# Two attention layers on one core: new tables of jobs, feed-forward products handed out in pairs, and a flag kept in a register

## What is computed

```python
x = L0_attn_x                       # (8, 512, 128)
xn = layernorm(x)
x = x + L0_attn(xn) + L0_ffn(xn)    # 16 heads, two softmax maps per head (dimension 4)
xn = layernorm(x)
x = x + L1_attn(xn) + L1_ffn(xn)    # 16 heads (dimension 8) with rotary positions

# L0_attn: o = softmax(q1 k1 / 2) v - lam * softmax(q2 k2 / 2) v; per-head rms norm; o @ W_proj + b
# L0_ffn:  both operands rounded to a 6-bit grid in blocks of 32 with a scale each, one product, bias
# L1_attn: softmax(rope(q) rope(k) / sqrt(8)) v; then @ w_proj
# L1_ffn:  h = 2 * relu(s0 * [x, -x] @ K0); h = 2 * relu(s1 * h @ K1); s2 * h @ K2
#          K0 (256 x 512), K1 (512 x 512), K2 (512 x 128) have entries +1 and -1
```

## Time and profile before

| what | us |
|---|---|
| median of three runs | 836.71 |
| the profiled execution, its own time | 837.15 |
| its span, first to last instruction | 835.4 |
| ACT busy | 760.7 (91% of the span) |
| PE busy | 749.4 (90%) |
| DVE busy | 551.5 (66%) |
| POOL busy | 64.2 (8%) |

### The profile page before, as it was taken

The page is one execution under the profiler, slowest core; times in us unless marked ns, Lnnn a source line. Parts: engine busy times, 40 slices in busy tenths (PEclk is TensorE's granted clock), DMA queues, the critical chain, the costliest instruction groups (busy, mean ns, idle before and its releaser), DMA issues.

```text
span 835.4 us, 17855 instructions
## 1 busy us (share of the span) xinstructions
PE 749.4 (90%) x6751; PEld 245.8 (29%) x6751; DVE 551.5 (66%) x1186; ACT 760.7 (91%) x856; POOL 64.2 (8%) x84
## 2 busy tenths in 40 slices
...
GB/s 104 182 38 176 77 90 194 73 2 76 140 75 129 14 77 139 103 102 14 115 133 138 33 52 140 82 159 2 102 128 81 122 2 123 81 1 88 128 13 14
DMA packets 45934, 73.99 MB, mean 89 GB/s; under 512 B 7344, under 2 KB 23344, under 8 KB 45712
## 3 DMA queue, kind: packets, MB, share of 16 engines
...
q10 hardware_dynamic: 64, 0.10, 0.0%
...
## 4 chain that ended last, share of the span: by engine, by line
PE 47%; ACT 29%; DVE 12%; issue 11%; DVEq 0%; DMA 0%; ACTq 0%; SPq 0%
ACT probs L807 28%; PE ps_pv L981 18%; PE ps_s L962 11%; PE ps_misc L828 6%; PE ps_misc L832 6%; PE ps_misc L833 4%; PE ps_misc L821 1%; ACT ff_out L759 1%; DVE pv_sb L1509 1%; DVE h_lo L1218 0%; ACT ff_out L761 0%; DVE tmp L1276 0%; DVE qk_rest L1269 0%; DVE qk_thirds L1266 0%; DVE xn L1093 0%
## 5 line engine op out<-in xcount | busy, mean ns | idle before, releaser
L807 ACT ACTIVATE probs<-ps_s 128x1024 f32<-128x1024 f32 x768 | 723.5, 1053 | 40.6 <-PE ps_s L962 40.0
L981 PE MATMUL ps_pv<-probs,v_aug 128*32 128x512 f32 x3072 | 411.4, 608 | 14.5 <-DVE pv_sb L1509 7.7
L962 PE MATMUL ps_s<-q_ab,k_ab 32*128 32x512 bf16 x896 | 88.9, 387 | 22.9 <-ACT probs L807 22.1
L962 PE MATMUL ps_s<-q_c,k_c 32*128 32x512 f32 (+1 forms) x640 | 81.0, 495 | 27.3 <-ACT probs L807 26.2
L981 PEld LDWEIGHTS ps_pv<-probs,v_aug 128*32 128x32 f32 x3072 | 61.7, 108 | 106.3 <-issue 79.1
L1216 DVE CAST h_hi<-ff_out 128x512 fp32r<-128x512 f32 x64 | 27.3, 427 | 93.7 <-ACT ff_out L759 91.2
L832 PE MATMUL ps_misc<-h_hi,k_w 128*128 128x512 f32 x192 | 85.9, 447 | 0.4 <-DVE tmp L1276 0.3
L1509 DVE STREAM_TRANSPOSE pv_sb<-ps_pv 128x512 f32<-128x512 f32 x48 | 34.4, 717 | 69.3 <-PE ps_pv L981 67.4
L833 PE MATMUL ps_misc<-h_lo,k_w 128*128 128x512 f32 x192 | 75.7, 395 | 0.0
L962 PEld LDWEIGHTS ps_s<-q_c,k_c 32*128 32x128 f32 (+1 forms) x640 | 30.9, 181 | 136.7 <-ACT probs L807 113.7
L962 PEld LDWEIGHTS ps_s<-q_ab,k_ab 32*128 32x128 bf16 x896 | 22.8, 91 | 158.6 <-ACT probs L807 127.0
...
## 6 DMA issues: line engine op xcount, KB each, us to landing
...
```

The costliest lines, as they stand in the source:

```text
L807: nc.scalar.activation(probs[:, U.slot(s), 2 * half:2 * half + 2], ps_s[:, 2 * pair:2 * pair + 2], ACT.Exp, bias=0.0 if U.first else -SCAL ...
L962: ins = nc.tensor.matmul(ps_s[:, bank, :], k[row:row + n, slot, c * P:(c + 1) * P], q[row:row + n, slot, :], start=True, stop=True)
L981: ins = nc.tensor.matmul(ps_pv[32 * j:32 * j + 32, :], v_aug[:, U.v, c, a:a + 32], probs[:, U.slot(s), j, :], start=c == 0 and not odd, st ...
```

## The change

The three tables are written anew. An item `ff1` or `ff2` is now one block (two matmuls) with its number in the item, and `ff1_b`, `ff2_b` are the last block alone; so each output is four items that may stand in different steps. Each waits only for the split of the block that it reads (`ff_split`), where before it waited for all four. PE loads layer 0's flag once and keeps it in a register, so `exact0` of sequences 1 to 7 only branches. In layer 1's general path (skipped with the given data) the masked copy of q goes to a part of `q_c` that is free, instead of `h1_hi`, after a wait that this needs, since `h1_hi` may now be read meanwhile. The tables, of which two items of `LOOP` stand for the rest, and the code:

```diff
 LOOP = [
-    12: [("bias", 1), ("quant_mm", 1)], 14: [("exact0", 1), ("ff2", -1)]},
+    12: [("bias", 1)],
+     13: [("quant_mm", 1)], 14: [("exact0", 1)], 15: [("regroup", 0, "B", 0), ("ff2", -1, 0)]},
...
+        def masked(way, b):
+
+            if way == 1:
+                slot = operands(unit("C", b))[2]
+                return q_c[:, slot:slot + PARTS]
+            return h0_hi if way == 0 else q_masked
...
                 elif name in ("ff1", "ff1_b"):
                     c = slice(args[0] * P, (args[0] + 1) * P)
-                    pe.wait_ge(ff_split, 2 * (2 * NF * b + NF))
-                    for f in ((0, 1) if name == "ff1" else (2, 3)):
-                        ins = products(ps, k1_w[:, f, c], h0_hi[:, f, :], h0_lo[:, f, :], f == 0, f == NF - 1)
+                    f = NF - 1 if name == "ff1_b" else args[1]
+                    pe.wait_ge(ff_split, 2 * (2 * NF * b + f + 1))
+                    ins = products(ps, k1_w[:, f, c], h0_hi[:, f, :], h0_lo[:, f, :], f == 0, f == NF - 1)
                 elif name in ("ff2", "ff2_b"):
-                    pe.wait_ge(ff_split, 2 * (2 * NF * b + 2 * NF))
-                    for f in ((0, 1) if name == "ff2" else (2, 3)):
-                        ins = products(ps, k2_w[:, f, :], h1_hi[:, f, :], h1_lo[:, f, :], f == 0, f == NF - 1)
+                    f = NF - 1 if name == "ff2_b" else args[0]
+                    pe.wait_ge(ff_split, 2 * (2 * NF * b + NF + f + 1))
+                    ins = products(ps, k2_w[:, f, :], h1_hi[:, f, :], h1_lo[:, f, :], f == 0, f == NF - 1)
...
+            weights_within = []
+
             def heads_within(layer, b):
 
                 if layer == 0:
+                    if weights_within:
+                        return weights_within[0]
                     pe.wait_ge(bound0_ops, BOUND0_OPS)
                 else:
                     pe.wait_ge(bound_ops, BOUND_OPS * (b + 1))
                 own_instruction(pe)
-                return pe.value_load(flag_of(layer, b))
+                flag = pe.value_load(flag_of(layer, b))
+                if layer == 0:
+                    weights_within.append(flag)
+                return flag
...
-                qm, k = ((h0_hi, qk_parts), (h1_hi, qk_parts), (q_masked, qk_thirds))[way]
+                qm, k = masked(way, b), qk_thirds if way == 2 else qk_parts
...
+                    slot = operands(unit("C", b))[2]
+                    before = unit("C", b - 2) if b > 1 else unit("BA"[b], 0)
+                    dve.wait_ge(scores_made, 2 * STEPS * (before.u + 1))
                     row_maxima(1, b)
...
-                    m, hi, lo = ps_misc[rows_, :], h1_hi[rows_, 0, :], h1_hi[rows_, 1, :]
+                    m, hi, lo = ps_misc[rows_, :], q_c[rows_, slot + 2, :], q_c[rows_, slot + 3, :]
```

More of the change, by code:

```diff
@@ L85 @@
 FIRST = [
[L86 to L96, removed]
[5 rows of a table removed]
-     10: [("regroup", 1, "B", 0)], 11: [("ff1_b", 0, 0)], 13: [("quant", 2, 0), ("quant", 2, 1), ("quant", 2, 2)],
-     14: [("quant", 2, 3), ("quant", 2, 4), ("ff1", 0, 1)], 15: [("quant", 2, 5), ("quant", 2, 6)]},
@@ L104 @@
-    {0: [("ff1_b", 0, 1)], 1: [("ff1", 0, 2), ("take", 1, "B", 1), ("ff1_b", 0, 2)], 2: [("regroup", 1, "B", 1)],
-     3: [("bias", 2), ("combine", 1, 0), ("combine", 1, 1), ("combine", 1, 2)], 4: [("quant_mm", 2)], 5: [("combine", 1, 3)],
[3 rows of a table removed]
+    {0: [("v0", 0)], 1: [("fast", 0, "k", 1)], 4: [("setup", 0)], 5: [("quant", 0, 0), ("quant", 0, 1)], 6: [("quant", 0, 2),
+     ("quant", 0, 3), ("quant", 0, 4)], 9: [("quant", 0, 5), ("take", 0, "A", 0)], 10: [("quant", 0, 6), ("quant_w", 0),
+     ("norm0", 1, 0)], 13: [("w_t", 0), ("norm0", 1, 1), ("norm0", 1, 2)], 14: [("quant_mm", 0), ("norm0", 1, 3)]},
@@ new lines @@
+    {0: [("norm0", 1, 4), ("regroup", 0, "A", 0), ("x_t0", 1), ("take", 0, "A", 1), ("regroup", 0, "A", 1), ("lambda", 0)],
+     1: [("bias", 0)], 2: [("q0", 1)], 3: [("quant", 1, 0)], 4: [("quant", 1, 1), ("quant", 1, 2), ("k0", 1)],
+     6: [("quant", 1, 3), ("quant", 1, 4)], 7: [("exact0", 1), ("take", 0, "B", 0)], 8: [("v0", 1)], 9: [("bias", 1)],
+     10: [("regroup", 0, "B", 0), ("quant", 1, 5)], 11: [("quant", 1, 6)], 13: [("quant_mm", 1), ("norm0", 2, 0)],
+     14: [("norm0", 2, 1), ("norm0", 2, 2), ("norm0", 2, 3)], 15: [("norm0", 2, 4), ("take", 0, "B", 1),
+     ("regroup", 0, "B", 1), ("combine", 0, 0)]},
@@ new lines @@
+    {1: [("x_t0", 2)], 2: [("combine", 0, 1)], 3: [("combine", 0, 2), ("q0", 2), ("combine", 0, 3), ("combine", 0, 4),
[8 rows of a table added]
+     14: [("quant", 2, 3), ("quant", 2, 4), ("ff1", 0, 1, 2)]},
+    {0: [("quant", 2, 5), ("quant", 2, 6), ("ff1_b", 0, 1)], 1: [("ff1", 0, 2, 0), ("ff1", 0, 2, 1), ("take", 1, "B", 1),
+     ("ff1", 0, 2, 2)], 2: [("ff1_b", 0, 2)], 3: [("regroup", 1, "B", 1), ("bias", 2), ("combine", 1, 0), ("combine", 1, 1),
+     ("quant_mm", 2)], 4: [("combine", 1, 2)], 5: [("combine", 1, 3)], 6: [("combine", 1, 4), ("combine", 1, 5),
[4 rows of a table added]
```

28 lines of the change are left out of this document (14 added, 14 removed), and 90 rows, old and new, of tables (FIRST, LAST, LOOP).

## The result

The changed kernel takes 824.22 us (median of 4 runs, 822.82 to 825.15) where the kernel before takes 837.27 beside it (4 runs, 836.52 to 837.96): 0.9846 of it, with a 95% interval of 0.9834 to 0.9857. The forecast was 823.0, in a range of 816 to 831. The profiled execution of after took 823.92, 13.23 less than that of before.

What follows compares the result with a forecast made beforehand. The prediction took ACT's pace to bound the kernel, with only PE's late score handovers (most of ACT's 40.6 us idle) to win. Terms -5.2 - 2.2 - 0.7 - 1.0 - 4.1 - 0.5 = -13.7 gave 823.0 us, range 816 to 831.

Steps and rivals of the forecast that it cites:

- The bodies: The four repeated bodies, units A, B and C: 1.3 us less each, -5.2 in all (-8.8 to +1.2).
- Unit B: In each body: `quant_mm` one step later no longer waits for `quant_t`, and one ff2 pair fits the cushion: -1.9 us.
- Unit C: In each body: ff2 pairs in steps 1 to 3 use up cushion, so v0 in step 4 finds less: +0.3 us.
- unit A: In each body: `exact1` beside the eight matmuls, with project1 ahead leaving no cushion: +0.3 us (0 to +0.7).
- The slow rival: In the bodies, DVE's in-order queue comes late at its takes and stalls PE as in B6: 848 us, chance 0.06.
- thin steps: Rival: feed-forward pairs standing apart cost PE like thick steps, so bodies gain about 0: 828 us, chance 0.12.
- The branch beside the eight matmuls: In the bodies' unit A: `exact1`'s flag and branch cost 0.21 us; a whole step's 1.83 each would make 7 worse.
- A0 and B0: First units: PE's 1.42 us wait for the copy of `wf_t` goes, `xn` costs 0.8 less: -2.2 (-1 to -3).
- B6 and A7: The take on DVE comes 2.4 us sooner, so PE's stall and its slow clock go: -4.1 (-1 to -5).
- B6 keeps a stall: Rival: the take or k0's part on DVE slips over 2 us past PE; stall and slow clock stay: 827, chance 0.08.
- B1 and C0: Three lone steps of four matmuls, 0.3 us each, are spread into pairs: -1.0 (0 to -1.5).
- C5 to C7: Late units: steps of eight matmuls become two, four and six, using more steps' cushions: -0.5 us (+0.5 to -1.5).

Runs made afterwards that it cites:

- e3: The kernel before, with only `quant_mm` moved one step later (12 to 13) in unit B of the four bodies: 831.74 us, 0.9936 of before.
- e4: The changed kernel, with only `quant_mm` put back to step 12 in unit B of the four bodies: 831.74 us, 0.9929 of before.
- e11: The changed kernel, with ff2 in the four bodies done as before, in thick steps (two items in step 14 of B, the rest in step 1 of C): 827.41 us.
- e5: The changed kernel, with PE loading layer 0's flag again each time, as before: 824.23 us, 0.9839 of before.
- e6: The changed kernel, with ff0(3) and project1 one step sooner in the bodies' unit A and `exact1` alone in step 12: 827.89 us, 0.9880 of before.
- e7: The changed kernel, with part 1 of the norm ahead of the copy of `wf_t` on DVE again in A0: 825.51 us, 0.9857 of before.
- e8: The changed kernel, with k0:7 and exact0:7 sooner in B6, last ff1 matmuls later, take ahead of bias, quantising parts 3 to 6 behind both: 818.49 us.
- e1: The kernel before, with only part 6 of the quantising put behind the take and its regrouping in B6: 838.82 us, 1.0021 of before.

## Why the prediction was right, and where it wasn't

*What bounds the kernel* holds: the idle time of ACT ahead of the exponentials fell to 29.2 (forecast "about 30"), 11.4 of the 13.2.

*The bodies* were -6.7 for -5.2. Unit B: -2.0 for -1.9, and e3, e4 and e11 show the two parts (1.4 for the wait on `quant_t`, 0.6 for the thick ff2 step, where I had 1.4 and 0.5). Unit C: +0.13 for +0.3, unit A +0.2 for +0.3. In unit C I had v0 find less cushion in step 4; its step is 2.01 long in C2 of after, where it was 2.19 (and is again in e11, which has the relu back in step 1). The relu now comes in step 3, just ahead of it, and ACT's longer step gives PE time to catch up.

*The slow rival* wasn't seen: no DVE take held PE back over the cushion in a body. Layer 0's flag is worth nothing, as said (e5). I had called thin steps a rival, at 0.12; e11 speaks against it.

*The branch beside the eight matmuls.* Its step lasts 3.57 in A3 against 3.30 in before, without it: 0.27 more, 0.36 by e6. Layer 1's flag is not kept in a register: PE still loads it each time, here at 306.91 for 0.30 (L942). Only 0.09 of the 0.27 shows in PE's own step, which takes 3.46 from scores to scores (306.85 to 310.31) where it took 3.37; the rest goes with the cushion that project1, in the step ahead, uses up. Beside four matmuls the trace of before had 0.21. The rule of the Trainium skill (Runtime: NRT & Kernel Launch, Instruction fetch mechanics) that a taken branch outside the fetched pages waits for a fetch is compatible with the difference, but no row here shows a fetch; a step's length was the bound I named, and 0.36 is a fifth of that.

*A0 and B0* came to -1.8 for -2.2, but not as worked out. I added 1.42 for `wf_t` and 0.8 for `xn` as if they were two waits (and 1.37 - 0.7 is 0.67, not 0.8; PE in fact waits 1.12 for `xn`). By e7 most of the first is the second seen sooner; the copy's place is worth 0.4. The other 1.4 is then due to the rest of the new order there, which wasn't tested.

*B6 and A7* is the step that failed: -4.1 predicted, -0.7 measured. "The stall goes, and with it the slow clock. Sum: -6.2" was right as far as B6's pv of step 10: that wait is gone and B6's clock is 1.00. The term "+0.3 for what may remain of the wait" was the wrong one. What stands next behind a stall of 4.56 has to be priced, and that was A7's load of q and k: 3.03 idle, and the slow clock moved one unit on (A7's granted clock is 0.95, and A7 is 1.2 shorter in e8, where it is 1.00). The distance from `qk_rest` to the first scores that can use it (17.5 in before) could have been read beside the time to A7's start. With the stall gone A7 would start 5 sooner, and k0's part on DVE is where it was. e1 and e8 show it from both sides: taking the take's stall alone away gains nothing, and putting both chains first gains 5.7. The rival *B6 keeps a stall* named k0's part on DVE as a way to it and had a chance of 0.08; the stall came, but its 827 did not, since other terms gave more than I had counted. The step that I feared there did not come: the take kept its 0.72 beside POOL's work.

*B1 and C0, C5 to C7.* -1.85 for -1.0 and -2.0 for -0.5 with B7 and the tail. The cause, that steps of eight became steps of two, four and six, was named, and I took too little for it: C7's worst steps lost 1.06, 1.18 and 0.61 over ACT's pace before and lose 0.74 and 0.97 in after (C7's steps 6, 7 and 9, and now 5 and 7). These sums are read from the traces and weren't isolated by a run.

So the time was right partly by luck, since errors cancel: 3.4 too much in B6 and A7 and 0.8 in the first three units, against 1.5, 0.85 and 1.5 too little in the bodies, in B1 and C0, and at the end.
